# A gated feed-forward with a median cut: the search's comparisons regrouped, two row buffers, sums and first loads of down issued sooner

## The reference

```python
s = jax.nn.silu(jnp.einsum('bsh,ih->bsi', x, w_gate))
k = int(0.5 * I)
_, idx = jax.lax.top_k(-jnp.abs(s), k)
flat = flat.at[rows, idx.reshape(B * S, k)].set(0.0)     # the half of smallest magnitude goes
s = s * jnp.einsum('bsh,ih->bsi', x, w_up)
return jnp.einsum('bsi,hi->bsh', s, w_down)
```

## Time and profile before

| | |
|---|---|
| median of 3 runs | 1415.43 us (1413.87 to 1415.97) |
| the profiled execution | 1412.86 us |
| its span, first to last instruction | 1410.9 us |
| mean granted TensorE clock | 0.988 of full |
| PE busy | 1362.0 us, 97% |
| DVE busy | 981.2 us, 70% |
| POOL busy | 929.2 us, 66% |
| ACT busy | 739.2 us, 52% |
| DMA, mean | 154 GB/s |

### The profile page before, as it was taken

The page is one execution under the profiler, slowest core; times in us unless marked ns, Lnnn a source line. Parts: engine busy times, 40 slices in busy tenths (PEclk is TensorE's granted clock), DMA queues, the critical chain, the costliest instruction groups (busy, mean ns, idle before and its releaser), DMA issues.

```text
span 1410.9 us, 30485 instructions
## 1 busy us (share of the span) xinstructions
PE 1362.0 (97%) x12727; PEld 1014.1 (72%) x12727; DVE 981.2 (70%) x1324; ACT 739.2 (52%) x935; POOL 929.2 (66%) x613
## 2 busy tenths in 40 slices
PE   4999999999999999899999999999997999999996
PEld 4555555555555555599999998888886888887874
DVE  6888888888888888870001899989898223255654
ACT  6788888888888888732224625243331111111211
POOL 0899888888888888813443343223233899999881
PEclk9999999999999999999999999999998999999998
DMA  9023323233333330024337348384736876855561
GB/s 357 33 104 102 136 97 114 99 117 104 117 98 121 100 107 18 16 77 169 139 124 299 122 164 276 126 294 126 275 104 244 299 258 189 272 186 181 160 202 45
DMA packets 110016, 217.62 MB, mean 154 GB/s; under 512 B 7200, under 2 KB 82864, under 8 KB 104880
## 3 DMA queue, kind: packets, MB, share of 16 engines
q1 hardware_dynamic: 88928, 192.89, 39.4%
q10 hardware_dynamic: 20944, 22.70, 5.1%
HBM read 173.63 MB, written 41.94 MB: 153 GB/s over the span
## 4 chain that ended last, share of the span: by engine, by line
PE 77%; DVE 13%; DMA 4%; ACT 3%; issue 2%; POOL 0%; DVEq 0%; ACTq 0%; SPq 0%
PE fast_psum L1896 16%; PE fast_psum L2033 16%; PE fast_psum L1914 15%; PE fast_psum L1981 14%; PE fast_psum L1933 6%; DVE fast_below L1392 4%; PE fast_psum L2003 2%; DMA fast_mag<-s 1%; PE fast_psum L1940 1%; PE fast_psum L2017 1%; PE fast_psum L2063 1%; DMA sk<-fast_sx 1%; PE fast_psum L2084 1%; PE fast_psum L1919 1%; DVE fast_near L1429 1%
## 5 line engine op out<-in xcount | busy, mean ns | idle before, releaser
L1322 DVE TENSOR_TENSOR fast_masked<-fast_psum,fast_mask_t 128x1024 f32<-128x1024 f32 (+1 forms) x416 | 488.2, 1218 | 72.0 <-PE fast_psum L1896 70.4
L1178 POOL TENSOR_TENSOR fast_pair<-fast_probs 128x1024 f32<-128x1024 f32 x192 | 457.0, 2383 | 96.1 <-PE fast_psum L1933 47.9
L1659 ACT ACTIVATE fast_probs<-fast_masked 128x1024 f32<-128x1024 f32 (+1 forms) x416 | 437.8, 1058 | 68.0 <-DVE fast_masked L1322 52.8
L1896 PE MATMUL fast_psum<-fast_qT,fast_kraw 32*128 32x256 f32 (+1 forms) x3328 | 245.7, 401 | 6.5 <-issue 3.3
L1914 PE MATMUL fast_psum<-fast_probs,fast_vraw 128*32 128x256 f32 (+1 forms) x3328 | 226.5, 386 | 0.8 <-ACT fast_probs L1659 0.8
L1896 PEld LDWEIGHTS fast_psum<-fast_qT,fast_kraw 32*128 32x128 f32 (+1 forms) x3328 | 152.9, 181 | 92.6 <-DVE fast_masked L1322 54.0
L1233 POOL TENSOR_TENSOR fast_d_lo<-fast_d_raw,fast_d_hi 128x256 fp32r<-128x256 f32 (+1 forms) x264 | 198.2, 781 | 5.3
L1209 POOL TENSOR_TENSOR fast_g_lo<-fast_g_raw,fast_g_hi 128x2816 fp32r<-128x2816 f32 x14 | 87.8, 6274 | 145.5 <-ACT fast_g_hi L1718 123.4
L1981 PE MATMUL fast_psum<-fast_g_hi,fast_z_hi 128*128 128x352 f32 x512 | 166.4, 325 | 1.8 <-POOL fast_g_lo L1209 1.8
L1981 PE MATMUL fast_psum<-fast_g_hi,fast_z_lo 128*128 128x352 f32 x512 | 165.5, 323 | 0.0
L1981 PE MATMUL fast_psum<-fast_g_lo,fast_z_hi 128*128 128x352 f32 x512 | 165.0, 322 | 0.0
(11 more groups left out here) (164 smaller groups left out, 1898.2 us busy)
## 6 DMA issues: line engine op xcount, KB each, us to landing
fast_d_raw<-w_down SPq DMA_DIRECT2D x63, 512.0 KB, 3.7
fast_kraw<-ctx_t SPq DMA_DIRECT2D x32, 800.5 KB, 6.0
fast_vraw<-ctx_nat SPq DMA_DIRECT2D x16, 1536.0 KB
fast_g_raw<-w_gate_up SPq DMA_DIRECT2D x15, 1408.0 KB, 7.3
fast_mag<-s SPq DMA_DIRECT2D x8, 1376.0 KB, 9.8
fast_sx<-s SPq DMA_DIRECT2D x8, 1376.0 KB, 6.8
sk<-fast_sx SPq DMA_DIRECT2D x8, 1376.0 KB, 7.1
fast_u_raw<-w_up_t SPq DMA_DIRECT2D x21, 512.0 KB, 5.4
```

Source lines behind the costliest of these rows:

```text
L1178: pool.tensor_tensor(pair[:, n % PAIR_BUFS], both[:, :, 0, :], both[:, :, 1, :], ALU.add).then_inc(paired, 1)
L1322: dve.tensor_tensor(into, of, m, ALU.add).then_inc(mask_added, 1)
L1659: act.activation(probs[0:r, g % RING, hp * HALF:(hp + 1) * HALF], masked[0:r, h % SLOTS, :], ACT.Exp).then_inc(exp_done, 1)
L1896: last = pe.matmul(scores[0:r, (2 * g + hp) % SLOTS, h % 2, i * 256:(i + 1) * 256], kraw[b % BUFS][q, u, c * P:c * P + r], qT[q, b, u, :], ...
```

## The change

Four things change, all within the search and around it.

- *Comparisons.* In pairs 1, 2 and 3 ScalarE compares rounds 0, 1 and 2 in one go, then two copies later rounds 3 and 4, then three copies later round 5. Those of pair 1 begin behind the last tile of gate. The sums of tiles 5, 6 and 7 stand behind copies 11, 17 and 23 instead of 12, 19 and 25.
- *Two row buffers.* `sx` has two buffers and, for the last tile, the place of `mag` of tile 5. `load_sx` waits for the store of the tile two before. `load_mag` now stands ahead of `load_sx` and `store_sk` in a turn.
- *Down's first transfers.* ScalarE issues `load_block` 0 and 1 and the four `load_u` after copy 34 instead of 40, when six tiles of `sk` are stored.
- *The last tile's store* moves from behind up into turn 19, ahead of down's first two weight loads; the store before it moves from turn 18 to 17. The slab's alignment goes from 512 to 128 bytes, which leaves every buffer at its address.

```diff
@@ -727,7 +727,7 @@
         H_HI = T_H + 2 * TW
         H_LO = H_HI + HS * TW
         OUT = H_LO + HS * TW
-        LINE = 512
+        LINE = 128
         sb("slab", [P, SLAB + LINE // 4], F32)
         base = -(-(nc.sbuf_base - 4 * SLAB - LINE) // LINE) * LINE
 
@@ -770,7 +770,8 @@
         mag = [at(f"mag{j}", WIDE + I * j, [I])[:, :] for j in range(MAGS)]
         near = at("near", WIDE + 3 * I, [I])[:, :]
         below = [at(f"below{j}", WIDE + 3 * I + I // 2 * j, [I], BF16)[:, :] for j in range(2)]
-        sx = at("sx", WIDE + 4 * I, [I])[:, :]
+        sx_of = [at(f"sx{j}", start, [I])[:, :] for j, start in enumerate((WIDE + 4 * I, THIN + 2 * HT * GJ))]
+        sx = [sx_of[t % 2] for t in range(TILES - 1)] + [mag[(TILES - 3) % MAGS]]
         t_sk = [at(f"t_sk{j}", THIN + 3 * BW * j, [3, BW]) for j in range(2)] + [
             at("t_sk2", Z_HI + D * 6 + DK * (E + ER), [3, BW])]
         t_u = [at(f"t_u{j}", T_U + TW * j, [TW]) for j in range(TURNS)]
@@ -817,8 +818,8 @@
         summed = sem("summed")
         step = sem("step")
         kept = sem("kept")
-        sx_full = sem("sx_full")
-        sk_stored = sem("sk_stored")
+        sx_full = [sem(f"sx_full{j}") for j in range(2)]
+        sk_stored = [sem(f"sk_stored{j}") for j in range(2)]
         sk_full = [sem(f"sk_full{j}") for j in range(BLOCKS)]
         tu_full = [sem(f"tu_full{j}") for j in range(TURNS)]
         t_turned = sem("t_turned")
@@ -939,13 +940,15 @@
 
         GATE_ABS_AT = {40: 0, 41: 1, 51: 2, 63: 3}
         GATE_COUNT_AT = {42: (0, 0), 44: (0, 1), 45: (0, 2), 46: (0, 3), 48: (0, 4), 49: (0, 5)}
-        UP_ABS_AT = {6: 4, 12: 5, 19: 6, 25: 7}
-        UP_COUNT_AT = {0: (1, 0), 1: (1, 1), 2: (1, 2), 3: (1, 3), 4: (1, 4), 5: (1, 5),
-                       13: (2, 0), 14: (2, 1), 15: (2, 2), 16: (2, 3), 17: (2, 4), 18: (2, 5),
-                       26: (3, 0), 27: (3, 1), 28: (3, 2), 29: (3, 3), 30: (3, 4), 31: (3, 5)}
+        GATE_COUNTS = {63: (1, (0, 1, 2))}
+        UP_ABS_AT = {6: 4, 11: 5, 17: 6, 23: 7}
+        UP_COUNT_AT = {1: (1, (3, 4)), 4: (1, (5,)),
+                       11: (2, (0, 1, 2)), 13: (2, (3, 4)), 16: (2, (5,)),
+                       23: (3, (0, 1, 2)), 25: (3, (3, 4)), 28: (3, (5,))}
         GATE_MAG_AT = {9: 2}
-        UP_SK_AT = {1: 1, 5: 2, 7: 3, 12: 4, 13: 5, 18: 6}
-        UP_MAG_AT = {0: 4, 5: 5, 7: 6, 12: 7}
+        UP_SK_AT = {1: 1, 5: 2, 7: 3, 11: 4, 13: 5, 17: 6, 19: 7}
+        UP_SX_AT = {0: 2, 2: 3, 6: 4, 8: 5, 12: 6, 13: 7}
+        UP_MAG_AT = {0: 4, 5: 5, 7: 6, 11: 7}
         LOAD_X_AT = {0: 0, 12: 1, 30: 2}
         MIX_W_AT = 24
 
@@ -1046,13 +1049,19 @@
                 sp.dma_start(mag[t % MAGS], s[t * P:(t + 1) * P, :]).then_inc(mag_full[t % MAGS], 16)
 
             def load_sx(t):
-                if t >= 1:
-                    sp.wait_ge(sk_stored, 16 * t)
-                sp.dma_start(sx, s[t * P:(t + 1) * P, :]).then_inc(sx_full, 16)
+                if t == 1:
+                    sp.wait_ge(g_lo_done, LOADS)
+                elif t == TILES - 1:
+                    sp.wait_ge(kept, t - 1)
+                elif t >= 2:
+                    sp.wait_ge(sk_stored[t % 2], 16 * (t // 2))
+                sp.dma_start(sx[t], s[t * P:(t + 1) * P, :]).then_inc(sx_full[t % 2], 16)
 
             def store_sk(t):
                 sp.wait_ge(kept, t + 1)
-                sp.dma_start(sk[t * P:(t + 1) * P, :], sx).then_inc(sk_stored, 16)
+                if t == TILES - 1:
+                    sp.wait_ge(sk_stored[t % 2], 16 * (t // 2))
+                sp.dma_start(sk[t * P:(t + 1) * P, :], sx[t]).then_inc(sk_stored[t % 2], 16)
 
             def load_down(n):
                 k = n % IC
@@ -1107,9 +1116,9 @@
                 if p == NCH + 2:
                     load_sx(0)
                 if p + 1 == PASSES:
+                    load_sx(1)
                     store_sk(0)
                     load_mag(3)
-                    load_sx(1)
                 store_gate(p)
                 if p == NCH:
                     sp.wait_ge(s_stored[0], 16 * (NCH // 2 + 1))
@@ -1122,19 +1131,18 @@
                 if f == 0:
                     for j in range(2):
                         sp.wait_ge(s_stored[j], 16 * NCH)
+                if f in UP_MAG_AT:
+                    load_mag(UP_MAG_AT[f])
+                if f in UP_SX_AT:
+                    load_sx(UP_SX_AT[f])
                 if f in UP_SK_AT:
                     store_sk(UP_SK_AT[f])
-                    if UP_SK_AT[f] + 1 < TILES:
-                        load_sx(UP_SK_AT[f] + 1)
-                if f in UP_MAG_AT:
-                    load_mag(UP_MAG_AT[f])
                 if f == UF - 2:
                     for n in range(2):
                         load_down(n)
                 store_up(f)
             sp.wait_ge(u_done, 2 * UF)
             load_down(2)
-            store_sk(TILES - 1)
             for n in range(STEPS):
                 if n + DS < STEPS:
                     load_down(n + DS)
@@ -1458,11 +1466,11 @@
             def keep(t):
 
                 dve.wait_ge(step, steps[0])
-                dve.wait_ge(sx_full, 16 * (t + 1))
-                done(dve.scalar_tensor_tensor(sx, near, thr[:, :], sx, ALU.is_ge, ALU.mult))
+                dve.wait_ge(sx_full[t % 2], 16 * (t // 2 + 1))
+                done(dve.scalar_tensor_tensor(sx[t], near, thr[:, :], sx[t], ALU.is_ge, ALU.mult))
                 dve.wait_ge(step, steps[0])
                 dve.wait_ge(rest_copied, t + 1)
-                dve.tensor_tensor(sx[:, UF * P:I], sx[:, UF * P:I], u_rest[:, t, :], ALU.mult).then_inc(kept, 1)
+                dve.tensor_tensor(sx[t][:, UF * P:I], sx[t][:, UF * P:I], u_rest[:, t, :], ALU.mult).then_inc(kept, 1)
 
             dve.wait_ge(iota_ready, 1)
             for p in range(PAIRS):
@@ -1754,11 +1762,17 @@
                     measure(GATE_ABS_AT[q])
                 if q in GATE_COUNT_AT:
                     compare(*GATE_COUNT_AT[q])
+                if q in GATE_COUNTS:
+                    p, rounds = GATE_COUNTS[q]
+                    for r in rounds:
+                        compare(p, r)
 
             def load_block(q):
                 gi, b = divmod(q, GB)
                 if b == 0:
-                    act.wait_ge(sk_stored, 16 * (GROUPS[gi][-1] + 1))
+                    stored = max(GROUPS[gi][-1] + 1, TILES - 2)
+                    for j in range(2):
+                        act.wait_ge(sk_stored[j], 16 * ((stored + 1 - j) // 2))
                 if q >= BLOCKS:
                     act.wait_ge(t_turned, 2 * (q - BLOCKS) + 2)
                 m, t0, w = len(GROUPS[gi]), GROUPS[gi][0], min(BW, I - b * BW)
@@ -1787,8 +1801,10 @@
                 if i in UP_ABS_AT:
                     measure(UP_ABS_AT[i])
                 if i in UP_COUNT_AT:
-                    compare(*UP_COUNT_AT[i])
-                if i == 2 * UF - 2:
+                    p, rounds = UP_COUNT_AT[i]
+                    for r in rounds:
+                        compare(p, r)
+                if i == 2 * UF - 8:
                     for q in range(2):
                         load_block(q)
                     for n in range(TURNS):
```

## The result

The changed kernel takes 1425.03 us in the median, the kernel before 1414.73 in the same comparison: a ratio of 1.007, 95% interval 1.005 to 1.0091. It is slower. One of the seven executions took 2704.15 us at a full granted clock; the ratio leaves it out, without it the median is 1424.8, and why it took so long is open. The profiled execution took 1428.07 us, its span is 1426.2, where before it was 1410.9. The forecast was 1413.6, within 0.2% of the time before, with a range that ended at 1419.

What follows compares the result with a forecast made beforehand. TensorE was taken as full except at 1074 to 1100, where it waits 6.7 us for sk. The seam's -7.4 and stalls' +5.6 gave -1.8 us: 1411.0 profiled, 1413.6 against the median, range 1408.5 to 1419.

Steps and rivals of the forecast that it cites:

- The seam at full clock: Between up and down: down's second step at 1087.7, 9.1 us saved; 7.4 with 1.65 taken off for a fallen clock.
- Waits for sums and sx gone: VectorE in up: waits of 3.55 and 3.25 us for ScalarE's sums and 0.96 for sx go.
- Pair 1 gives 0: Search in up: tile 3 done at 928.7 with or without sums moved; bounds 1.9 and 1 gained, or 3 lost.
- the lock to GpSimd's period: Search rounds in up: a VectorE that has caught up waits for GpSimd's next split, once per 10.88 us.
- about 4.4 remain: Pair 2 in up: collisions of VectorE with GpSimd's splits, 9 us before, fall to about 4.4; sixth tile at 997.
- R + 12.1 us: Up: from a pair's first comparison, at R, 12.1 us pass until TensorE goes on after the copy.
- Group 28 5.6 us late in all: Up: waiting for copy 24, group 28 starts at 1009.4, due 1003.8; 5.6 late, group 16's 2.5 included.
- Clock loss 0: Up: a clock fallen behind the second stall would add matmul time; counted as 0, bounds 0 and 3 us.
- u_raw worth 0: Up's weight loads, issued later: covered with 1 to 4 us to spare, worth 0; without that cover up to 4.
- TensorE waits for copies: Rival at group 28, behind copy 24: sixth tile at 1001.4, stall 10 us, time 1419.7 to 1421; chance 0.2.
- The search catches up: Rival in up's search: few collisions, sixth tile by 992, only the first 2.5 us stall remains, 1408.8; chance 0.2.
- Down's weights keep the seam: Rival at down's start: last tile ends at 1080, weights ready at 1093, nothing changes, 1415.4; chance 0.1.

Runs made afterwards that it cites:

- experiment 1: The changed kernel with comparisons one at a time, each behind its own copy, and sums at their old copies: 1409.15 us, 0.9967 of the kernel before.
- experiment 3: The changed kernel with the load of u_raw for turn f + 3 issued ahead of turn f's two stores: 1423.86 us, 1.0066 of the kernel before.
- experiment 4: The changed kernel with the grouped comparisons of pairs 2 and 3 later, behind copies 14 and 27 first, sums unmoved: 1419.29 us, 1.0034 of before.

## Why the prediction was wrong, point by point

- **The seam at full clock, 9.1 us:** right, 9.7, and 9.4 in experiment 1, where TensorE's delay doesn't help. The clock that I took off, 1.65, was not lost: down's first step takes 4.33, 0.19 over the normal 4.14.
- **Waits for sums and sx gone:** right. VectorE has no wait for a sum in up.
- **Pair 1 gives 0, tile 3 done at 928.7:** the lock to GpSimd's period exists, and experiment 3 shows it: VectorE's long instructions in the rounds of pair 1 are one period apart there (11.0 and 10.9 us), and the next guess begins at 929.58.

```profile
865.04 1.41 DVE L1417 TENSOR_TENSOR fast_db<-fast_cut 128x2 f32<-128x2 f32 x1
...
876.08 1.26 DVE L1417 TENSOR_TENSOR fast_db<-fast_cut 128x2 f32<-128x2 f32 x1
...
886.95 1.27 DVE L1417 TENSOR_TENSOR fast_db<-fast_cut 128x2 f32<-128x2 f32 x1
```

  But the period was taken as a clock of its own, "once per 10.88 us", and the splits were followed from where they lay before. In the changed kernel they don't lie there: the grouping moves the copies, these the stores, these the load, and the meetings are at 865.88, 877.54 and 890.31. Tile 3 was done at 932.7, and the next pair's first guess took 2.31 us. The bound of "3 lost where a split shifts into a bad phase" was there (up began 0.9 us later in this execution), and I took the 0.
- **Pair 2, "about 4.4 remain":** this is the step that failed. I reasoned that GpSimd has nothing to split while TensorE stalls. True for rounds 0 to 2; then the late copies bring splits into rounds 3 and 5 (6.0 us), and the guess (2.1) and the tiles' work (6.8) meet others that I had not followed. The pair took 14.6 us more than the clean 64.2. My upper bound, 9 as before, was too low by 5.6, because I took the length of before as the worst case while the change moved what that length is made of.
- **R + 12.1 us until TensorE goes on:** right to 0.12 us. The comparisons stood at 935.15 and 1013.91; the sum gives 947.25 and 1026.0, TensorE went on at 947.37 and 1026.12. With R as forecast, 929.0 and 997.3, the stalls would have been mine; R was late by 6.1 and 16.6.
- **Group 28 5.6 us late in all:** it was due at 852.42 + 28 x 5.44 = 1004.74 and came at 1026.12, 21.4 late: 7.6 and 11.4 of stalls, 1.9 of clock between them, 0.5 not accounted for.
- **Clock loss 0, bounds 0 and 3:** as I had set it up, the first stall's loss (1.9) only shortens the second stall, and the second's is added: 1.8, inside the bound. But the 0 was wrong. The trace of before had shown a fallen clock behind 6.66 us of idle time, and stalls of 7.6 and 11.4 are longer.
- **u_raw worth 0:** right for TensorE, which never waited for a split here, and wrong as a step: it was the load by which the collisions came about, and in experiment 4 it became the wait.
- **The rivals:** "TensorE waits for copies" is what happened, at its place, and it too was priced with pair 2 at its old length: 1421 where 1425 was measured. "The search catches up" is what the run without reading splits shows. "Down's weights keep the seam" did not come: GpSimd had split them by 1101.6, before up ended. Its sign, a first split of d after 1085, did appear (1093.78), and it meant nothing with an end of up at 1104.

In sum, for the profiled execution: -9.7 + 19.0 + 3.7 + 0.9, where the forecast had -7.4 + 5.6.
